# Second edge-network pass of a graph network: one-hots issued one step earlier in VectorE's order

## The reference, cut to what matters

```python
for s in range(S):                                   # S = 2
    ce = jnp.concatenate([e, n[senders], n[receivers]], axis=-1)
    e = e + _ln(_mlp(ce, edge_blk_w0[s], edge_blk_b0[s], edge_blk_w1[s], edge_blk_b1[s]), ...)
    agg = jax.ops.segment_sum(e.astype(jnp.float32), receivers, num_segments=num_nodes)
    ...
```

## Time and profile before

| | us |
|---|---|
| median of 3 runs | 19862.05 (19857.42 to 19865.26) |
| the profiled execution | 19815.21 |
| its span | 19813.6 |
| second edge-network pass within it | about 14,070 to 17,450 |

### The profile page before, as it was taken

One profiled execution on the slowest core, in us unless ns is written; L12 is line 12 of the kernel. 1 busy time (PEld: TensorE's weight loads), 2 busy tenths in 40 slices (PEclk: granted clock), 3 DMA queues, 4 the chain that ended last, 5 costly groups with the idle time before them and its releaser, 6 DMA issues. The chain is left out here.

```text
span 19813.6 us, 553798 instructions
## 1 busy us (share of the span) xinstructions
PE 15287.0 (77%) x200647; PEld 13589.7 (69%) x201524; DVE 13621.7 (69%) x32754; ACT 8118.3 (41%) x17256; POOL 5755.4 (29%) x4543
## 2 busy tenths in 40 slices
PE   2666666666666997799999999997688888856665
PEld 1666666666664996688888888886566666646565
DVE  3777777777775997555555555554677777769899
ACT  0444444444442332355555555553344444421111
POOL 1888888888880110011111111110000000001111
PEclk9555555555555997899999999998899999977676
DMA  2222222222222553344444444443344444427676
GB/s 56 54 54 50 53 54 54 54 52 52 54 51 66 157 157 91 91 110 110 110 110 108 112 109 111 108 111 80 114 139 139 140 142 139 139 61 210 173 209 181
DMA packets 1402755, 2062.56 MB, mean 104 GB/s; under 512 B 764952, under 2 KB 938022, under 8 KB 1359282
## 3 DMA queue, kind: packets, MB, share of 16 engines
q1 hardware_dynamic: 1089098, 1709.41, 27.8%
q0 software_dynamic: 218240, 197.29, 9.1%
q10 hardware_dynamic: 94544, 142.53, 2.0%
HBM read 1521.71 MB, written 523.16 MB: 103 GB/s over the span
## 5 line engine op out<-in xcount | busy, mean ns | idle before, releaser
L759 POOL DMA_INDIRECT records<-e_sort_rec,e_sort_index x3300 | 4328.5, 1312 | 1063.8 <-issue 989.5
L2442 POOL DMA_DIRECT2D states<-e_s_second_t x550 | 475.4, 864 | 4685.2 <-ACT e_s_second_t L2139 4342.2
L1088 PE MATMUL e_sort_acc<-e_sort_thirds,e_sort_hot 128*128 128x48 f32 x7260 | 1574.6, 414 | 320.8 <-DVE e_sort_hot L918 320.8
L1088 PEld LDWEIGHTS e_sort_acc<-e_sort_thirds,e_sort_hot 128*128 128x128 f32 x7260 | 1556.9, 332 | 353.2 <-DVE e_sort_hot L918 353.2
L2284 PE MATMUL e_s_ps_g<-e_s_parts,e_s_pick 128*128 128x64 bf16 x32670 | 1419.9, 198 | 276.0 <-DVE e_s_g_sb L1943 256.0
L2433 POOL DMA_INDIRECT e_s_spill<-send,e_s_lists x220 | 299.9, 1363 | 4257.3 <-PE e_s_ps_h L2344 3214.0
L2284 PEld LDWEIGHTS e_s_ps_g<-e_s_parts,e_s_pick 128*128 128x128 bf16 x32670 | 1301.5, 101 | 339.2 <-DVE e_s_g_sb L1943 290.8
L1943 DVE COPY e_s_g_sb<-e_s_ps_g 128x512 f32<-128x512 f32 x440 | 303.5, 690 | 1483.6 <-PE e_s_ps_h L2303 1376.5
L1926 DVE TENSOR_SCALAR e_s_pick<-e_s_rows,lane_below 128x1024 bf16<-128x1024 bf16 (+1 forms) x3300 | 1247.5, 436 | 3.2 <-PE e_s_ps_h L2326 3.1
L1005 ACT ACTIVATE e_sort_away<-iota,e_sort_slots 128x128 f32<-128x128 f32 x3850 | 1171.0, 388 | 10.7
L2354 PEld LDWEIGHTS e_s_ps_o<-w_eblk,e_s_act 128*128 128x128 f32 x7920 | 1040.8, 192 | 169.8 <-issue 146.5
(11 more groups left out here) (548 smaller groups left out, 37148.2 us busy)
## 6 DMA issues: line engine op xcount, KB each, us to landing
e_s_rows<-rows_d SPq DMA_DIRECT2D x330, 1088.0 KB, 5.3
e_s_hot<-hots_d SPq DMA_DIRECT2D x550, 560.0 KB, 3.9
e_s_to_rows<-rows_d SPq DMA_DIRECT2D x220, 608.0 KB, 5.4
e_s_rows<-rows_d SPq DMA_DIRECT2D x220, 544.0 KB, 4.1
e_s_rows<-rows_d SPq DMA_DIRECT2D x220, 512.0 KB
e_s_to_rows<-rows_d SPq DMA_DIRECT2D x220, 512.0 KB
states<-e_s_first_t ACTq DMA_DIRECT2D x440, 256.0 KB
states<-e_s_second_t POOLq DMA_DIRECT2D x440, 256.0 KB
```

Source lines behind the costliest of these rows:

```text
L759: pool.indirect_dma_start(records, bass.IndirectOffsetOnAxis(ap=index[x][:, t:t + 1], axis=0), rec[x][:, t, :], None,).then_inc(written[x] ...
L1088: mm = pe.matmul(acc[c // ACC][:, c % ACC * SPAN * F:(c % ACC + 1) * SPAN * F], hot[:, c, :], thirds[:, c, :, :].rearrange("p h f -> p (h ...
```

## The change

In VectorE's `body`, for the second pass alone (`not enc`), `picks` of groups 2, 3 and 4 is issued in step s = 0, 1 and 2, in place of s = 1, 2 and 3. It stays at the head of its step, so it now stands ahead of `norm1` of that step, and the first of them ahead of `merge` too. The first pass keeps its order. No instruction is added or dropped.

```diff
                 for s in G_ALL:
+                    if not enc and main and s < NG - 2:
+                        picks(k - 1, y, s + 2, before - 1)
                     if main and enc:
                         norm0(k - 1, y, s)
                     if enc and main and s:
                         gathered_(k - 1, y, s - 1, before - 1)
-                    if main and 1 <= s < NG - 1:
+                    if enc and main and 1 <= s < NG - 1:
                         picks(k - 1, y, s + 1, before - 1)
                     if out_:
                         norm1(k - 2, x, s)
                     if before >= 3 and s == 0:
                         merge(k - 3, y, before - 3)
```

## The result

| | before | after |
|---|---|---|
| median of 4 runs, us | 19863.65 | 19623.96 (19618.04 to 19632.83) |
| ratio after / before | | 0.9879, 95% interval 0.9864 to 0.9894 |
| span of the profiled execution, us | 19813.6 | 19631.2 |
| second pass, first to last gather matmul, us | 14074.2 to 17433.3: 3359.1 | 14122.4 to 17249.8: 3127.4 |

The change saves 240 us by the medians. The pass itself is 231.7 us shorter.

A forecast was written before the change was run, and what follows sets the result against it. A chain of waits through VectorE's one-hots for group 2's gather, closing once per block, bounds the pass. 173 us from it plus 35 of clock make 208, giving 19654 us; narrow range 19625 to 19680, 8-in-10 range 19590 to 19745.

The forecast's parts named there:

- The chain through group 2's one-hots: VectorE's path from group 0's gather start (P) to group 2's (G): 1.6 us a block, 108 times, 173 us.
- The next bound: TensorE's first hidden layer of group 0, ending within 0.1 us of the moved one-hots, caps the gain at 1.78 a block.
- The clock: TensorE's slow-clock stretches, 33 in the pass costing 43 us: 35 us expected back, bounds 0 and 50.
- The moved norm and merge: Norm 0 and merge on VectorE come 1.59 us later, hidden by idle time and ScalarE's slack; priced at nothing.
- Groups 3 and 4 gain nothing: Their gathers on TensorE never waited, so issuing their one-hots earlier on VectorE gains nothing.
- The clock recovered: Rival 1, 18%: TensorE's clock doesn't recover, only the 173 us come, 19689.
- the states took nothing: Rival 2, 12%: the states' transfer takes over TensorE's wait, half the gain goes, 86 us, 19776.
- the norms were not the path: Rival 4, 3%: later norms delay ScalarE's split and activation, up to 1.59 us a block, 172 us slower, 20034.
- the fourth: The slower rival, 3%: the norms are the path through ScalarE, 20034.
- The signs: Blocks 28.7 to 29.2 us, TensorE's one-hot wait under 0.5, last-sums wait 1.33, VectorE's split wait about 5, clock 0.99 or 1.00.

The follow-up runs named there:

- states_first: From the changed kernel, SyncE issues the states of groups 0 and 1 ahead of the one-hot patterns for the sums; 19596.24 us, ratio to before 0.9878.
- before_roots: From the changed kernel, group 2's one-hots go further up, ahead of the roots; 19559.37 us, ratio to before 0.9858.
- both_ends: From the changed kernel, states of groups 0 and 1 ahead of the patterns and group 2's one-hots ahead of the roots; 19530.59 us, ratio to before 0.9849.
- g23_first: From the changed kernel, one-hots of groups 2 and 3 both ahead of norm 0 and merge, group 4's in step 2; 19586.63 us, ratio to before 0.9874.
- g34_alone: Against the kernel before, only the one-hots of groups 3 and 4 come one step earlier, group 2's stay; 19866.90 us, ratio 0.9996.
- group4_back: From the kernel with states ahead of patterns and group 2's one-hots ahead of the roots, group 4's return to step 3; 19586.85 us, ratio to before 0.9858.
- merge_ahead: Against the changed kernel, step 0 runs the merge, then group 2's one-hots, then norm 0; 19823.01 us, ratio to before 0.9975.
- below_norm: Against the changed kernel, group 2's one-hots stand ahead of the merge but behind norm 0; 19709.17 us, ratio to before 0.9915.
- g2_alone: Against the kernel before, only group 2's one-hots move ahead of norm 0 and merge; 19638.56 us, ratio 0.9881.

## Why the prediction was right

It named 19654, and 19624 was measured, 1 us below the narrow range that it gave itself (19625 to 19680) and inside the wide one. It had 208 us of gain; the pass gave 231.7, and the medians 8 more, which the spread of the runs covers.

- **The chain through group 2's one-hots, 173 us.** Right in place, a little small in size. P to G fell by 9.13 - 7.40 = 1.73, or 187 us for 108 blocks. I had taken 1.6, the 1.65 with something off for late states. Instead up to 0.12 came on top, because the one-hots start sooner behind the roots than the norm does. The next bound was named rightly for half of the bodies: one-hots and first hidden layer end 7.21 and 7.23 behind P, in the mean, in bodies without the jump. Behind the jump they end at 7.38 and 6.78, and there the one-hots alone still bound. states_first, before_roots and both_ends show both sides.
- **The clock, 35 of 43 us.** All 33 stretches went: G to sums fell from 20.94 to 20.54, 0.40 x 108 = 43 us. The count and the price were right, the share that stays away was too small. The count was luck: the rows left 25 to 42 stretches open, and the lower end was taken without a reason. That the stretches would go was an expectation too; no row of before could show it. The two terms give 230 of the 231.7 us.
- **The moved norm and merge, at nothing.** Right: the first activation ends at G + 1.7 (I said 2.0, wanted 3.96), the first sums start at G + 8.7 without a wait, VectorE still idles 3.5 to 3.8 before the fourth `less0`. I had said 2.6, by taking the whole 1.65 off the 4.22. But my own list had the row end only 1.0 later (G + 9.4 for 8.4), and it ended at G + 9.0: a wait of 0.80 before the third `less0` took part of the delay. g23_first doubled the delay for nothing; both_ends found the end of the slack.
- **Groups 3 and 4 gain nothing.** Right, by g34_alone.
- **The rivals.** The clock recovered, the states took nothing (0.36 a block of wait as against 0.34 before), and the norms were not the path. Under the fourth I gave ScalarE's 4.34 as a sign that nothing overtakes in a queue. That row doesn't show it, since the activation behind had its input only at 46.76. The rows of after do: the input is there at 52.67, the split ahead waits for its norm until 53.09, and the activation starts at 53.62.
- **The signs.** All waits came out as written. The block of 28.57 is just under the 28.7 to 29.2 that I gave, for the two sizes above.

## What to carry to other kernels

If an engine that looks busy for 86% stands once per turn, follow the one instruction that it waits for back along the other engine's queue, and add up what stands ahead of it without being needed first: that sum, cut at the next thing that is late, is the gain. Look at the two ends of such a wait before moving more; here two causes tied within 0.1 us in every second body, and a move of either alone gave 1.5 to 27 us where both gave 73. Check the granted clock in every candidate, since a better order with the idle time at another place can lose more by the clock than it wins: group4_back won 15 us from G to the last sums over both_ends and lost 39 in slow first gathers.

## What the runs showed of the hardware

The slow stretches of TensorE don't follow the length of a wait evenly. The wait between first hidden layer and third gather varies within each kernel. In before it was 1.49 to 2.69 us, and 27 of the 92 third gathers read were slow. In merge_ahead it was 0.48 to 2.19, and 37 were slow. In below_norm it was up to 1.58, and none was, though in merge_ahead waits from 0.99 on had a slow gather behind them. Nor does chance scatter them: in before the slow third gathers stand 3, 3 and 4 blocks apart, over and over, from the second hit to the end of the pass, with slow and normal ones behind waits of the same length. So where in time the wait falls counts beside its length. The runs don't show by what rule, and it stays open why merge_ahead was hit more often than before.

The wait before the last sums tells the same. At 1.33 us it made 0 to 7 first gathers of a pass slow in after, g2_alone, below_norm, g23_first, states_first, before_roots and both_ends. In group4_back it was 1.35 to 1.53 ahead of the first gathers that were slow. All slow first gathers stood in bodies behind the loop's jump, where 0.26 to 0.33 of idle time follow the last sums. Of the 46 such bodies read in group4_back, none of the 10 with a wait of 1.33 or 1.34 was slow, and 21 of the 36 with a longer one were. Part of the longer wait comes from the first cast of the window tables on VectorE (L1987). It took 0.28 to 0.35 us in half of that kernel's blocks and 0.22 in all blocks of after and both_ends; why, no run separates. The Trainium skill ("TensorE: Matmul & The Clock Gate", HAM oscillation) tells of a kernel in which every burst of matmuls behind a DMA wait starts slow. Its waits, about 3 to 5 us, are longer than any of these, and here none to under half of the bursts did.

The loop's jump shows, once the loop has run a few turns, as a gap on VectorE of 0.41 to 0.52 us behind the roots and on TensorE as 0.26 to 0.32 before the first gather, in every second body. The two blocks of a turn are written one after the other, and the unrolled blocks behind the loop don't have the gap. The profile puts it down to whatever semaphore stands behind it: to the roots where the norm comes first (0.43 in before), to TensorE's gather where the one-hots do (0.41 in after). In merge_ahead, where the merge comes first, it is 0.52 and no releaser is named.
